# A convolution by diagonal matmuls, a stage without GpSimd, and gating placed behind each split

## The reference

```python
x_in = (x @ in_proj_w.T)[..., :512]                     # 256 -> 512 channels
xc   = causal depthwise conv of x_in, 4 taps per channel, + conv_b
u    = silu(xc)
x_dbl = u @ x_proj_w.T                                  # 33 rows: dt_raw, B (16), C (16)
dt   = clip(softplus(dt_raw @ dt_proj_w.T + dt_proj_b), 1e-4, 10)
# the scan takes u, dt, dt*u, B and C
```

## Time and profile before

| | |
|---|---|
| median of 3 runs | 6604.36 us (6603.5 to 6609.78) |
| profiled execution | 6595.66 us; span from the first to the last instruction 6593.9 us |
| mean TensorE clock granted | 0.799 of 2.4 GHz |
| busy: TensorE, VectorE, ScalarE, GpSimd | 5250.2, 4847.6, 3841.4, 1359.9 us |
| `ssm_input_phase` | from 3712.1 us to 4403.3 us of the span: 691.2 us, or 10.5% |

### The profile page before, as it was taken

One profiled execution on the slowest core, in us unless ns is written; L12 is line 12 of the kernel. 1 busy time (PEld: TensorE's weight loads), 2 busy tenths in 40 slices (PEclk: granted clock), 3 DMA queues, 4 the chain that ended last, 5 costly groups with the idle time before them and its releaser, 6 DMA issues. The chain is left out here.

```text
span 6593.9 us, 95276 instructions
## 1 busy us (share of the span) xinstructions
PE 5250.2 (80%) x27420; PEld 2038.0 (31%) x27420; DVE 4847.6 (74%) x9319; ACT 3841.4 (58%) x6353; POOL 1359.9 (21%) x1658
## 2 busy tenths in 40 slices
PE   6979799797979889795999744428888888887778
PEld 3333333333332332333666422201111111114555
DVE  6666564756656575765888688879999999986768
ACT  5555555555555555553444466657777777774443
POOL 0000000000000000000111144443333333334421
PEclk8989899898989989897999866655555555558999
DMA  0000000000000000001111133331111111114432
GB/s 23 1 14 1 14 1 1 14 1 14 1 14 1 8 7 1 7 1 31 40 42 42 57 116 116 110 109 44 44 44 44 45 45 45 45 40 158 152 96 70
DMA packets 198907, 273.60 MB, mean 41 GB/s; under 512 B 13989, under 2 KB 157989, under 8 KB 192454
## 3 DMA queue, kind: packets, MB, share of 16 engines
q1 hardware_dynamic: 181190, 252.90, 12.6%
q10 hardware_dynamic: 17408, 16.78, 0.7%
HBM read 151.14 MB, written 118.49 MB: 41 GB/s over the span
## 5 line engine op out<-in xcount | busy, mean ns | idle before, releaser
L643 DVE TENSOR_REDUCE at_nmax<-at_ps_s 128x1 f32<-128x1024 f32 x1024 | 1248.2, 1224 | 641.9 <-PE at_ps_s L342 640.6
L485 ACT ACTIVATE at_probsT<-at_ps_t 128x512 f32<-128x512 f32 x2048 | 1111.4, 595 | 832.1 <-PE at_ps_t L367 832.0
L2035 DVE SCALAR_TENSOR_TENSOR sc_decayed<-sc_da,sc_state 128x256 f32<-128x256 f32 x2048 | 776.8, 425 | 139.5 <-ACT sc_da L1990 138.6
L1990 ACT ACTIVATE sc_da<-sc_da,sc_a_col 128x1024 f32<-128x1024 f32 x512 | 559.7, 1093 | 346.6 <-PE sc_da L1926 346.6
L2045 DVE CUSTOM_DVE_ANT_0 sc_state<-sc_xd,sc_decayed 128x256 f32<-128x256 f32 x2048 | 756.3, 409 | 1.5 <-DVE sc_decayed L2035 1.5
L1902 POOL TENSOR_SCALAR sc_xd<-sc_xd 128x1024 f32<-128x1024 f32 x512 | 532.2, 1039 | 958.1 <-ACT sc_xd L1997 958.1
L1938 PE MATMUL sc_ps_du<-sc_parts,sc_sel 24*128 24x512 bf16 x1024 | 565.4, 609 | 201.7 <-ACT sc_xd L1997 201.7
L363 PE MATMUL at_ps_t<-at_qkT 108*128 108x512 bf16 x2048 | 664.2, 385 | 65.1 <-ACT at_probsT L485 35.6
L342 PE MATMUL at_ps_s<-at_qkT 108*128 108x512 bf16 x2048 | 666.7, 410 | 26.3 <-DVE at_nmax L643 12.2
L1997 ACT ACTIVATE sc_xd<-sc_ps_du,sc_bt 128x512 f32<-128x512 f32 x1024 | 651.2, 695 | 5.7 <-PE sc_ps_du L1938 5.7
L376 PE MATMUL at_ps_o<-at_probsT,at_v 128*32 128x256 f32 x8192 | 628.3, 390 | 1.4 <-ACT at_probsT L485 1.4
(11 more groups left out here) (307 smaller groups left out, 7972.7 us busy)
## 6 DMA issues: line engine op xcount, KB each, us to landing
dt_parts<-si_pt SPq DMA_DIRECT2D x64, 384.0 KB, 2.6
du_parts<-si_pu SPq DMA_DIRECT2D x64, 384.0 KB, 3.2
sc_parts<-dt_parts SPq DMA_DIRECT2D x128, 192.0 KB
sc_parts<-du_parts SPq DMA_DIRECT2D x128, 192.0 KB
u_tok<-si_ut SPq DMA_DIRECT2D x8, 2048.0 KB, 8.3
y<-sc_yo SPq DMA_DIRECT2D x256, 64.0 KB
so_yin<-y SPq DMA_DIRECT2D x32, 512.0 KB
so_uin<-u_tok SPq DMA_DIRECT2D x32, 512.0 KB
```

The source lines that it names most:

```text
L485: nc.scalar.activation(probsT[:, c % RING, u * HALF:(u + 1) * HALF], ps_t[u][:], ACT.Exp).then_inc(s_exp, 1)
L643: nc.vector.tensor_reduce(nmax[:, par, t:t + 1], ps_s[t % 2][:], AX_X, ALU.max, negate=True).then_inc(s_max, 1)
L1990: nc.scalar.activation(flat, flat, ACT.Exp, scale=a_col[:]).then_inc(s_da, 1)
L2035: nc.vector.scalar_tensor_tensor(decayed[:, ch], da[q % 2][:, j % 2, ch], DECAY_MIN, state[:, (j - 1) % SRING, ch], ALU.max, ALU.mult).the ...
```

## The change

The convolution moves to TensorE: VectorE builds once 16 diagonal matrices of 128 x 128 (`taps`, one per group and tap), and for each bank `n` TensorE accumulates four matmuls of such a diagonal with `xc` shifted by 0 to 3 tokens. The bias goes into Silu, which now reads PSUM. GpSimd is left with one `memset`: 1 + exp becomes a ScalarE Copy with bias 1, the subtractions of the first parts (`rests`) go to VectorE. `dt` and `du` get 4 buffers instead of 2, `third_parts` come one block later, and on ScalarE each `split(b-1, t)` is followed by one gating of 512 tokens of batch b, while `bc_stored` and all `u_stored` of batch b stand behind the last split.

```diff
+            def convolved(b, m):
+                pe.wait_ge(s_xc, b * 8 + 2 * m + 2)
+                for hf in range(NHALF):
+                    n = m * NHALF + hf
+                    if n >= 4:
+                        pe.wait_ge(s_u, b * 8 + n - 3)
+                    for j in range(CONV):
+                        last = nc.tensor.matmul(ps[n % 4][:], taps[:, m, j, :],
+                                                xc[:, m, j + hf * HALF:j + (hf + 1) * HALF],
+                                                start=(j == 0), stop=(j == CONV - 1))
+                    last.then_inc(s_conv, 1)
...
+                    if m >= 1:
+                        convolved(b, m - 1)
+                convolved(b, KI - 1)
                 for hf in range(NHALF):
                     for m in range(KI):
-                        if hf == 0:
-                            pe.wait_ge(s_u, b * KI + m + 1)
+                        if hf == 0 and m in (0, KI - 1):
+                            pe.wait_ge(s_u, b * 8 + (6 if m == 0 else 8))
...
-            def gated(b):
-                for m in range(KI):
-                    act.wait_ge(s_conv, KI * b + m + 1)
-                    nc.scalar.activation(u[:, m], acc[:, m], ACT.Silu).then_inc(s_u, 1)
+            def gated(b, n):
+                m, hf = n // NHALF, n % NHALF
+                act.wait_ge(s_conv, 2 * KI * b + n + 1)
+                nc.scalar.activation(u[:, m, hf * HALF:(hf + 1) * HALF], ps[n % 4][:], ACT.Silu,
+                                     bias=cb[:, m:m + 1]).then_inc(s_u, 1)
...
                 for t in range(TB):
+                    nc.scalar.activation(ex1[:, t], ex[:, t], ACT.Copy, bias=1.0).then_inc(s_ex1, 1)
                     nc.scalar.activation(lg[:, t], ex[:, t], ACT.Ln, bias=1.0).then_inc(s_lg, 1)
...
                 logs(b - 1)
-                gated(b)
                 for t in range(TB):
                     split(b - 1, t)
-                    if t == 2:
-                        bc_stored(b)
-                        act.wait_ge(s_stu, 16 * b)
-                    if t >= 3:
-                        u_stored(b, t - 3)
-                for t in range(TB - 3, TB):
+                    gated(b, t)
+                bc_stored(b)
+                act.wait_ge(s_stu, 16 * b)
+                for t in range(TB):
                     u_stored(b, t)
...
+            def rests(b, t):
+                w, r, i = t % 2, t % RING, b * TB + t
+                dve.wait_ge(s_t1, i + 1)
+                nc.vector.tensor_tensor(dt[:, r], dt[:, r], pt[:, w, 0], ALU.subtract).then_inc(s_tr, 1)
+                dve.wait_ge(s_u1, i + 1)
+                nc.vector.tensor_tensor(du[:, r], du[:, r], pu[:, w, 0], ALU.subtract).then_inc(s_ur, 1)
...
-                for t in range(1, TB):
-                    products(b, t)
-                    third_parts(b, t - 1)
-                third_parts(b, TB - 1)
-
-            conv(0)
+                for t in range(1, TB + 2):
+                    if t < TB:
+                        products(b, t)
+                    if t <= TB:
+                        rests(b, t - 1)
+                    if t >= 2:
+                        third_parts(b, t - 2)
```

More of the change, by code:

```diff
@@ L1367, in ssm_input_phase @@
     identf, _ = ident
+    RING = 4
     B, T, D, TB, KD, DI, KI, S, CONV = sh.B, sh.T, sh.D, sh.TB, sh.KD, sh.DI, sh.KI, sh.S, sh.CONV
@@ L1385, in ssm_input_phase @@
         xT = sb("xT", [P, KD, T])
-        one_col = sb("one_col", [P, 1])
+        taps = sb("taps", [P, KI, CONV, P])
         xc = sb("xc", [P, KI, PAD + T])
-        acc = sb("acc", [P, KI, T])
         u = sb("u", [P, KI, T])
@@ L1395, in ssm_input_phase @@
         lg = sb("lg", [P, TB, DI])
-        dt = sb("dt", [P, 2, DI])
-        du = sb("du", [P, 2, DI])
+        dt = sb("dt", [P, RING, DI])
+        du = sb("du", [P, RING, DI])
         ut = sb("ut", [P, TB, DI])
@@ L1407, in ssm_input_phase @@
         s_zero = sem("pads_cleared")
+        s_taps = sem("taps_ready")
         s_x = sem("x_loaded")
@@ L1422, in ssm_input_phase @@
         s_arg = sem("softplus_arg_ready")
-        s_ex = sem("softplus_exp_ready")
         s_lg = sem("softplus_log_ready")
@@ L1495, in _ @@
             nc.gpsimd.memset(xc[:, :, 0:PAD], 0.0).then_inc(s_zero, 1)
[L1496 to L1509, removed]
         @block.tensor
@@ L1522, in _ @@
             pe.wait_ge(s_wr, 3)
+            pe.wait_ge(s_zero, 1)
+            pe.wait_ge(s_taps, 1)
+            def convolved(b, m):
[9 more added lines that the diff above has]
+                    last.then_inc(s_conv, 1)
             with pe.Fori(0, B) as b:
@@ L1610, in exps @@
                 act.drain()
-                nc.scalar.activation(ex[:, t], ex[:, t], ACT.Exp, scale=-1.0).then_inc(s_ex, 1)
+                nc.scalar.activation(ex[:, t], ex[:, t], ACT.Exp, scale=-1.0)
             def logs(b):
@@ L1623, in split @@
                 act.wait_ge(s_std[w], b * TB * 8 + t // 2 * 16)
-                nc.scalar.copy(pt[:, w, 0], dt[:, w]).then_inc(s_t1, 1)
-                nc.scalar.copy(pu[:, w, 0], du[:, w]).then_inc(s_u1, 1)
+                nc.scalar.copy(pt[:, w, 0], dt[:, r]).then_inc(s_t1, 1)
+                nc.scalar.copy(pu[:, w, 0], du[:, r]).then_inc(s_u1, 1)
                 act.wait_ge(s_tr, i + 1)
-                nc.scalar.copy(pt[:, w, 1], dt[:, w]).then_inc(s_t2, 1)
+                nc.scalar.copy(pt[:, w, 1], dt[:, r]).then_inc(s_t2, 1)
                 act.wait_ge(s_ur, i + 1)
-                nc.scalar.copy(pu[:, w, 1], du[:, w]).then_inc(s_u2, 1)
+                nc.scalar.copy(pu[:, w, 1], du[:, r]).then_inc(s_u2, 1)
             x_stored(0)
@@ L1633, in _ @@
                 projected(0, m)
-            gated(0)
+            for n in range(2 * KI):
+                gated(0, n)
             bc_stored(0)
@@ L1663, in _ @@
             dve.wait_ge(s_w, 7 * 16)
[L1664 to L1676, removed]
+            for m in range(KI):
+                for j in range(CONV):
+                    last = nc.vector.tensor_scalar(taps[:, m, j, :], identf[:], cw[:, m, j:j + 1], None, ALU.mult)
+            last.then_inc(s_taps, 1)
             def dt_taken(b):
@@ L1700, in products @@
             def products(b, t):
-                w, i = t % 2, b * TB + t
+                w, i = t % RING, b * TB + t
                 dve.wait_ge(s_raised, i + 1)
@@ L1714, in products @@
                 nc.vector.tensor_tensor(du[:, w], dt[:, w], ut[:, t], ALU.mult).then_inc(s_du, 1)
+            def rests(b, t):
+                w, r, i = t % 2, t % RING, b * TB + t
+                dve.wait_ge(s_t1, i + 1)
+                nc.vector.tensor_tensor(dt[:, r], dt[:, r], pt[:, w, 0], ALU.subtract).then_inc(s_tr, 1)
+                dve.wait_ge(s_u1, i + 1)
+                nc.vector.tensor_tensor(du[:, r], du[:, r], pu[:, w, 0], ALU.subtract).then_inc(s_ur, 1)
             def third_parts(b, t):
-                w, i = t % 2, b * TB + t
+                w, r, i = t % 2, t % RING, b * TB + t
+                dve.wait_ge(s_tr, i + 1)
+                dve.wait_ge(s_ur, i + 1)
                 dve.wait_ge(s_t2, i + 1)
-                nc.vector.tensor_tensor(pt[:, w, 2], dt[:, w], pt[:, w, 1], ALU.subtract).then_inc(s_t3, 1)
+                nc.vector.tensor_tensor(pt[:, w, 2], dt[:, r], pt[:, w, 1], ALU.subtract).then_inc(s_t3, 1)
                 dve.wait_ge(s_u2, i + 1)
-                nc.vector.tensor_tensor(pu[:, w, 2], du[:, w], pu[:, w, 1], ALU.subtract).then_inc(s_u3, 1)
+                nc.vector.tensor_tensor(pu[:, w, 2], du[:, r], pu[:, w, 1], ALU.subtract).then_inc(s_u3, 1)
             def tokens(b):
@@ L1735, in _ @@
                 arguments()
-                conv(b)
                 tokens(b - 1)
```

1 line of the change is left out of this document (removed).

## The result

| | before | changed kernel |
|---|---|---|
| median | 6603.93 us (4 runs, 6594.9 to 6609.78) | 6756.69 us (4 runs, 6753.98 to 6766.06) |
| ratio to before | | 1.0238, 95% interval 1.0225 to 1.0251 |
| profiled execution | 6595.66 us, span 6593.9 | 6758.86 us, span 6757.1 |
| `ssm_input_phase` in the span | 3712.1 to 4403.3: 691.2 us | 3716.5 to 4569.8: 853.3 us |

The change makes the kernel 2.4% slower. The two profiled executions differ by 163.2 us, and 162.1 us of that lie in the phase that was changed; the medians differ by 152.8 us. The phase is the better ruler in what follows: in the profiled executions of this study the identical code ahead of it ended anywhere between 3709 and 3726 us, and the code behind it took between 2187 and 2192 us.

What follows compares the result with a forecast made beforehand. The prediction took the order of waits, no longer VectorE, to bound the changed phase. Batch 0 +19.1, six periods +116.2, batch 7 +19.8 and after the last batch +7.0 gave +162 us, a median near 6766 us, range 6700 to 6825.

Steps and rivals of the forecast that it cites:

- T: The moment of a batch's first projection on TensorE, recurring once per batch; the prediction counts its steps from it.
- first cast: ScalarE's first cast of a batch's eight token blocks, behind the logarithms; forecast at T + 41.0, was T + 34.8.
- stride of the blocks: Time from one token block to the next; forecast 6.44 us, of which 1.3 us wait on the store.
- six periods: Six spans from T to T, batches 1 to 7; 101.4 us each against 82.03, together +116.2 us.
- batch 0: First batch, without splits, where banks 4 to 7 wait for the first gating; 58.2 against 39.02 us, +19.1.
- batch 7 up to its exps: Last batch from T until its exps start; forecast 99.4 against 79.6 us, +19.8.
- the store loop: With two `pu` buffers and later third parts, each split waits for the store of two blocks before; 1.3 us per stride.
- the bare tail: `x_proj`, `u` transposes, copies and next input's transposes stand uncovered behind the last gating; 14.1 us to next T.
- Rival 1: The store doesn't close the loop of the blocks; stride is VectorE's 5.14 us, 52 us less, 6714 us; chance 10%.
- rival 2: TensorE's convolution ahead of the last projection runs at the slow clock, 1.2 GHz; 6876 us, half of it 6821; 9%.
- Rival 3: VectorE's relief decides and the kernel is faster; period 56 instead of 82 us, 6422 us; chance 5%.
- rival 4: No change: stride falls to 5.14 us, tail overlaps by half, the rest by a faster start; 6600 us; chance 2%.

Runs made afterwards that it cites:

- e1: Changed kernel with four instead of two buffers for the bf16 parts, three instead of four of `dt` and `du`; 6680.65 us, 1.0119 of before.
- e2: Changed kernel with third parts straight behind the rests of their block, two buffers of bf16 parts kept; 6681.95 us, 1.0125 of before.
- e3: Changed kernel with all eight projections of a batch ahead of the convolution on TensorE; 6672.3 us, 1.0115 of before.
- e9: Changed kernel with one convolution tap instead of four, 8 instead of 32 diagonal matmuls per batch; 6679.91 us, 1.0129 of before.
- e4: Changed kernel with two gatings behind each of the first four splits, instead of one behind every split; 6727.24 us, 1.0194 of before.
- e5: Changed kernel with third parts earlier, all projections ahead of the convolution and gatings in pairs, together; 6548.23 us, 0.9924 of before.
- e6: Kernel before with GpSimd's work moved to ScalarE and VectorE, convolution and gating left as they were; 6567.33 us, 0.9944 of before.
- e8: Changed kernel with the 1 + exp Copies moved from between the logarithms to behind the next block's Exp; 6767.0 us, 1.0255 of before.

## Why the prediction was right

Step by step, from the profile after (T of batches 0, 1 and 7: 3732.33, 3791.08, 4399.25):

| step | forecast | measured |
|---|---|---|
| last projection ends | T + 27.7 | T + 27.7 |
| first cast | T + 41.0 | T + 40.6 |
| stride of the blocks | 6.44 | 6.48 |
| first cast to end of last gating | 46.3 | 46.7 |
| last gating to next T | 14.1 | 14.1 |
| six periods | +116.2 | +116.0 |
| batch 0 | +19.1 | +19.7 |
| batch 7 up to its exps | +19.8 | +17.9 |
| after the last batch | +7.0 | +7.8 |
| start of the phase to T | 0 | +0.7 |
| sum | +162 | +162.1 |

That the sum agrees so closely is luck: batch 7 and the periods came out 2.1 us shorter, batch 0, the end and the start 2.1 us longer. The forecast of the median, 6766 us, was 9 us too high, because it let the median lie 8.7 us above the profiled execution, as before; it lay 2.2 us below.

Batch 0 came out as built from rows: the banks 4 to 7 behind the first gating (2.77 us of waiting) and then `x_proj`. The diagonals delayed the first transposes by 1.1 us, within the bounds given. Batch 7 was 1.9 us shorter: its last ten `x_proj` records began at T + 86.4 instead of the 87.3 of batch 4, and took 6.06 us instead of the 6.81 of the earlier trace rows.

The mechanisms were tested apart: the store loop (e1, e2), the convolution's place (e3, e9), the bare tail (e4, e5), the relief of VectorE (e6). Rival 1 and rival 2 fell in the trace: casts do wait for the store, and the convolution records ahead of the last projection ran at 0.43 us; the slow clock did show between the gatings (24 records in 13.39 us at 4039.42), where it is not on the chain. Rival 3, that VectorE's relief decides, fell: even in e5, which is faster than before, the period is 71.7 us and not 56, and VectorE waits 20.57 us of it for the first logarithm. With a sum of +162, rival 4, no change, fell too.

The slow clock is on the chain in one place that the prediction priced without naming it, the last ten `x_proj` records of a batch. They wait for the last gating:

```profile
3879.15 7.23 PE L1553 MATMUL si_ps<-si_u,si_xpT 128*33 128x512 f32 x10 [8.05 <-ACT si_u L1597]
3980.98 5.82 PE L1553 MATMUL si_ps<-si_u,si_xpT 128*33 128x512 f32 x10 [7.62 <-ACT si_u L1597]
```

In one batch of e2 the same ten took 4.48 us. The prediction called the run from `x_proj` to T warm, but the 6.81 us that it took from batch 0 held the slow records already; in the batch shown above the granted clock was 0.65 over their 6.80 us. So the clock costs about 2 us a batch here, and it is most of the reason why the periods vary from 100.4 to 102.6 us.

One reading of mine was wrong without harm: I wrote of the Copies that nothing hides them. The first cast did come at T + 41, but VectorE's first two products, which end 0.8 us before the first rest can start, ran beside them, as e8 shows. So the eight Copies, 4.2 us of ScalarE, had a price of at most some 1.3 us a batch (the estimate under e8), and not the 4.2.

On the table load between the first two splits:

```profile
4036.66 0.62 ACT L1635 CAST si_pu<-si_du 128x512 bf16<-128x512 f32 x1
4037.30 1.28 ACT L1597 ACT_TABLE_LOAD   x1
4038.59 0.69 ACT L1597 ACTIVATE si_u<-si_ps,si_cb 128x512 f32<-128x512 f32 x1
```

It takes 1.28 us with 0.02 us ahead and 0.01 behind. The Trainium skill, ScalarE: Activation LUTs, What ACT_TABLE_LOAD costs, adds a drain of 1.38 us. The trace shows none here, and the period, measured at 101.36 against a forecast of 101.4 without a drain, leaves no room for it.

## What to carry to other kernels

Relieving the engine with the most busy time (VectorE, from 73 to 47 us a batch) doesn't by itself shorten the period: follow one recurring instruction through a period, and cost the new order by its waits. When a step of a ring is put one place later, count again how long its buffers now wait for the store behind it; here 0.18 us of waiting per block were bought off with 1.3 us. Work given to an idle engine goes behind what another engine's list waits for, not ahead of it: the same 32 matmul records cost 12.6 us a batch ahead of the last projections (periods of 101.36 and 88.80 us); behind them TensorE was done 5 us before the gating that it waited for next.

## What the runs showed of the hardware

- A subtraction of VectorE with both inputs in SBUF took 1.64 us beside GpSimd and 0.68 alone; over the phase, L1705 had a mean of 1.400 us before and its successor L1701 0.684 after.
- An fp32 matmul of 128 x 128 by 512 columns is two records, 0.43 us apart with the clock granted in full (1.00 from 4001 to 4008 in the changed kernel, 16 records in 7.03 us), also with diagonal matrices as weights.
- TensorE's clock is a side effect of the order: where its list ran dry ahead of the projections (e4), sixteen records took 9.26 us instead of 7.13, about a quarter of what the shorter tail had won.
